# Leaves of six trees instead of four fetched by row, scaled rows of two trees added on VectorE before TensorE turns them, and one TensorE signal for each pair of halves

## The reference

```
h  = patches @ W.T + b                                   # 768 -> 256
x  = layernorm(h);  xn = x / max(rms(x), eps) * g
uv = silu(xn @ uv_w.T)                                   # u 512, v 512, base 128
q, k = rope(base * gamma + beta)
kernel = square(relu((q @ k.T + w_rel[j - i]) / sqrt(128)))
h  = h + x * res_scale + (u * (kernel @ v)) @ o_w.T
y  = layernorm(h)
logits = y @ W_in.T + b_in                               # 8 trees of 255 nodes
current = 0
for d in range(7):                                       # walk down each tree
    current = child of current, right where logits[current] > 0
acts = silu(logits) where the node was visited, else 0
out = h + acts @ W_out.T
```

## Time and profile before

| | us |
|---|---|
| median of 3 runs (least, most) | 2202.95 (2196.44, 2209.55) |
| profiled execution, its own time | 2201.36 |
| its span in the trace | 2199.5 |
| PE busy | 2066.1 (94%) |
| DVE busy | 1621.5 (74%) |
| ACT busy | 1395.2 (63%) |
| POOL busy | 774.1 (35%) |

### The profile page before, as it was taken

How to read it: one execution, slowest core, us unless ns; L and a number is a source line. 1 busy time by engine, 2 the same in 40 slices (tenths; PEclk the granted TensorE clock), 3 DMA queues, 4 the chain that set the end, 5 groups by cost and what they waited for, 6 DMA issues and landing times.

```text
span 2199.5 us, 42461 instructions
## 1 busy us (share of the span) xinstructions
PE 2066.1 (94%) x13256; PEld 1941.8 (88%) x13256; DVE 1621.5 (74%) x4210; ACT 1395.2 (63%) x3085; POOL 774.1 (35%) x905
## 2 busy tenths in 40 slices
PE   6899999999999999999999999999999999999997
PEld 5789889899988898888998898988889988889887
DVE  5678777777777787777777777777777877777775
ACT  5556666666666566566666665666665666656654
POOL 2752333232333333332323333323323233333233
PEclk8999999999999999999999999999999999999999
DMA  5331322222322223222223222222223232222222
GB/s 146 85 94 52 89 73 66 73 76 63 83 71 65 81 55 84 75 64 73 77 62 84 70 73 73 64 75 77 65 70 84 55 85 69 73 73 66 63 67 74
DMA packets 81999, 163.13 MB, mean 74 GB/s; under 512 B 17102, under 2 KB 48048, under 8 KB 81968
## 3 DMA queue, kind: packets, MB, share of 16 engines
q0 software_dynamic: 40960, 103.02, 17.4%
q1 hardware_dynamic: 41008, 59.71, 9.3%
HBM read 148.76 MB, written 13.90 MB: 74 GB/s over the span
## 4 chain that ended last, share of the span: by engine, by line
PE 84%; another core or an unknown queue 5%; ACT 4%; POOL 3%; issue 2%; DVE 1%; DMA 1%; ACTq 0%; POOLq 0%; SPq 0%; DVEq 0%
PE front L1142 10%; PE front L1144 9%; PE front L1143 9%; PE hid_ps L1142 9%; PE hid_ps L1143 9%; PE hid_ps L1144 9%; PE out_acc L1142 6%; PE out_acc L1143 6%; PE out_acc L1144 6%; PE out_acc L1378 4%; PE front L1177 2%; PE front L1184 2%; PE hid_ps L1366 2%; PE hid_ps L1337 2%
## 5 line engine op out<-in xcount | busy, mean ns | idle before, releaser
L474 POOL DMA_INDIRECT leaf_rows<-leaf_table,leaf_at x512 | 532.4, 1040 | 163.9 <-issue 163.4
L453 POOL TENSOR_TENSOR inv_root<-to_root,minus_half 98x8 f32<-98x8 f32 x64 | 111.0, 1734 | 728.3 <-DVE to_root L885 404.6
L528 ACT ACTIVATE hid_hi<-hid 128x392 fp32r<-128x392 f32 (+1 forms) x256 | 177.8, 695 | 237.1 <-PE out_acc L1144 155.4
L1142 PE MATMUL out_acc<-hid_hi,outw_lo 128*128 128x392 f32 x768 | 293.4, 382 | 2.6 <-DVE hid_lo L835 2.3
L1142 PE MATMUL hid_ps<-ffn_x,in_lo 128*128 128x392 f32 x768 | 282.3, 368 | 6.2 <-POOL in_lo L445 5.8
L1143 PE MATMUL hid_ps<-ffn_x,in_hi 128*128 128x392 f32 x768 | 266.3, 347 | 0.0
L1144 PE MATMUL hid_ps<-ffn_x,in_hi 128*128 128x392 f32 x768 | 264.7, 345 | 0.0
L1144 PE MATMUL out_acc<-hid_hi,outw_hi 128*128 128x392 f32 x768 | 264.6, 345 | 0.0
L1143 PE MATMUL out_acc<-hid_lo,outw_hi 128*128 128x392 f32 x768 | 264.4, 344 | 0.0
L473 POOL TENSOR_TENSOR held<-minus_half 98x1 f32<-98x1 f32 x128 | 47.2, 369 | 489.9 <-issue 428.7
L718 ACT ACTIVATE leaf_rows<-leaf_rows,leaf_act 98x256 f32<-98x256 f32 x512 | 218.2, 508 | 0.1
(11 more groups left out here) (140 smaller groups left out, 5808.2 us busy)
## 6 DMA issues: line engine op xcount, KB each, us to landing
x_raw<-x SPq DMA_DIRECT2D x192, 196.0 KB, 2.4
out<-out_stage SPq DMA_DIRECT2D x32, 392.0 KB
leaf_rows<-leaf_table,leaf_at POOLq DMA_INDIRECT x512
leaf_table<-leaf_rows SPq DMA_DIRECT2D x4, 256.5 KB, 4.7
out_stage<-in_w SPq DMA_DIRECT2D x4, 256.0 KB
tok_major<-tok_w SPq DMA_DIRECT2D x3, 256.0 KB, 4.3
late_raw<-out_w SPq DMA_DIRECT2D x6, 128.0 KB
u<-uv_w SPq DMA_DIRECT2D x1, 576.0 KB, 4.2
```

What stands on the lines that cost most here:

```text
L453: pool.tensor_tensor(inv_root[:, 0:size], to_root[:, 0:size], minus_half[:, 0:size], ALU.pow).then_inc(roots_ok, 1)
L474: pool.indirect_dma_start(row_slot(s, g), None, table, bass.IndirectOffsetOnAxis(ap=leaf_at[:, s, g:g + 1], axis=0), element_offset=s * P ...
L528: act.activation(out, src, ACT.Copy).then_inc(done, 1)
L1142: pe.matmul(out, w[1], x_parts[0], start=start, stop=False)
```

## The change

- `GATHERED` is 6 instead of 4, and the rows have 12 slots instead of 8. Two more trees leave out their leaf half in logits and out, and go through `find_leaf`, `leaf_number`, `fetch_rows`, `leaf_dots`, `leaf_silu`.
- Trees of fetched leaves go in couples. ACT scales the rows of the even tree only; DVE's new `merge_rows` (`scalar_tensor_tensor`, 98x256, one for each group) multiplies the odd tree's rows by their activation and adds the even tree's scaled rows; PE's `add_rows` runs once for each couple. A fetch into a slot waits for `rows_merged` where the even tree's rows lay there, for `rows_added` where the odd one's did.
- One signal for a pair of halves: `turn_h`, `turn_back` and `tree_out` raise their semaphore after m = 1 only, `tree_logits` after the last half; `embed` raises `x_used` only after k = 2 and k = 5, so `x_high(3)` waits for `embed(2)` and not for `embed(0)`.
- The lists of all engines are written anew: PE's list starts at another place of the same cycle, and 2 or 3 neighbours are exchanged in many places. POOL's list has `norm_roots` in other places.

```diff
-GATHERED = 4
+GATHERED = 6
-ROW_SLOTS = 8
+COUPLES = GATHERED // 2
+ROW_SLOTS = 12
+X_SIGNALS = (2, 5)
...
                     if GROUPS * (s + 1) > ROW_SLOTS or not first(i):
-                        pool.wait_ge(rows_added, GATHERED * i + s + 1 - ROW_SLOTS // GROUPS)
+                        couple = COUPLES * i + (s - ROW_SLOTS // GROUPS) // 2 + 1
+                        if (s - ROW_SLOTS // GROUPS) % 2 == 0:
+                            pool.wait_ge(rows_merged, GROUPS * couple)
+                        else:
+                            pool.wait_ge(rows_added, couple)
...
                 if k >= XRING or not first(n):
-                    act.wait_ge(x_used, n * XC + k - XRING + 1)
+                    act.wait_ge(x_used, 2 * n + k // XRING)
...
-                dve.wait_ge(h_turned, 2 * (2 * n + which) + m + 1)
+                dve.wait_ge(h_turned, 2 * n + which + 1)
...
+            def merge_rows(i, s):
+
+                if i is None:
+                    return
+                dve.wait_ge(leaf_active, GATHERED * i + s + 1)
+                dve.wait_ge(rows_scaled, GROUPS * (COUPLES * i + s // 2 + 1))
+                for g in range(GROUPS):
+                    one, two = (row_slot(n, g)[:, ROW_IN:ROW] for n in (s - 1, s))
+                    dve.scalar_tensor_tensor(two, two, leaf_act[:, s, g:g + 1], one,
+                                             ALU.mult, ALU.add).then_inc(rows_merged, 1)
...
-                last.then_inc(x_used, 1)
+                if k in X_SIGNALS:
+                    last.then_inc(x_used, 1)
...
-                last.then_inc(done, 1)
+                if m == DC - 1:
+                    last.then_inc(done, 1)
...
-                last.then_inc(logits_ready, 1)
+                if b == halves(t) - 1:
+                    last.then_inc(logits_ready, 1)
...
-                last.then_inc(tree_added, 1)
+                if m == DC - 1:
+                    last.then_inc(tree_added, 1)
...
-                pe.wait_ge(rows_scaled, GROUPS * (GATHERED * i + s + 1))
+                pe.wait_ge(rows_merged, GROUPS * (COUPLES * i + s // 2 + 1))
```

More of the change, by code:

```diff
@@ L1450, in body @@
+                tree_out(i, 0, 0)
+                find_leaf(i, 2)
+                make_base(n)
+                tree_logits(i, 5, 0)
+                tree_out(i, 0, 1)
+                tree_visits(i, 4)
+                make_v(n, 0)
+                make_v(n, 1)
+                make_v(n, 2)
+                tree_out(i, 1, 0)
+                make_v(n, 3)
+                find_leaf(i, 3)
+                tree_out(i, 1, 1)
+                tree_out(i, 2, 0)
+                tree_out(i, 2, 1)
                 if first(n):
@@ new lines, in body @@
+                add_rows(i, 1)
+                tree_logits(i, 6, 1)
+                tree_logits(i, 7, 0)
+                make_u(n, 2)
+                tree_visits(i, 6)
+                find_leaf(i, 5)
+                tree_out(i, 3, 0)
+                make_u(n, 3)
+                mix(n, 0)
+                mix(n, 1)
+                mix(n, 2)
+                tree_out(i, 3, 1)
+                mix(n, 3)
+                tree_logits(i, 7, 1)
+                tree_out(i, 4, 0)
+                tree_out(i, 4, 1)
@@ new lines, in body @@
+                project_o(n, 0, range(0, 3))
+                project_o(n, 0, range(3, EC))
+                project_o(n, 1, range(0, EC))
+                embed(nx, 0)
+                turn_h(n, 1, 0)
+                turn_h(n, 1, 1)
+                embed(nx, 1)
+                embed(nx, 2)
+                tree_visits(i, 7)
+                embed(nx, 3)
+                embed(nx, 4)
+                embed(nx, 5)
+                turn_ffn_x(n, 0)
+                turn_ffn_x(n, 1)
+                tree_out(i, 5, 0)
@@ new lines, in body @@
+                tree_out(i, 5, 1)
+                tree_out(i, 6, 0)
+                turn_h(nx, 0, 0)
+                turn_h(nx, 0, 1)
+                tree_logits(n, 0, 0)
+                tree_logits(n, 1, 0)
+                add_rows(i, 3)
+                tree_visits(n, 0)
+                tree_out(i, 6, 1)
+                tree_visits(n, 1)
+                tree_logits(n, 2, 0)
+                find_leaf(n, 0)
+                tree_logits(n, 3, 0)
+                add_rows(i, 5)
+                tree_out(i, 7, 0)
@@ L1476, in _ @@
+                tree_out(i, 7, 1)
+                turn_xn(nx, 0)
+                turn_xn(nx, 1)
             body(None, None, None, 0)
```

283 lines of the change are left out of this document (117 added, 166 removed).

## The result

The changed kernel takes 2314.76 us, the median of 4 runs (2312.09 to 2317.07), against 2203.7 for the kernel before: a ratio of 1.0505, 95% interval 1.0472 to 1.0539. It is 5% slower where 6% faster was forecast, and 239 us above the predicted 2076.

What follows compares the result with a forecast made beforehand. PE was taken as the bound: 58.8 us of work plus 4.1 of waits make a period of 62.9. 64.8 + 31 x 62.9 + 59.1 + 1.9 = 2075.7, so 2076 us was predicted, range 2020 to 2145.

Steps and rivals of the forecast that it cites:

- PE's work, 58.8: PE's busy time per pair after the change, in us, down from 63.4 with 24 fewer logits and out matmuls.
- turn_xn and make_base: 0.4 each: PE's waits per pair at these two steps, 0.4 us each, bounded by nothing and 1.36.
- How late a signal can be: Lateness of TensorE's signals in the stretch around make_base and make_v, put between 0.04 and 3.07 us.
- The cause of the lateness: TensorE's signals near make_base were said to come 1.8 to 3.1 us late behind the output store.
- Fewer signals: Joined TensorE signals: no gain in ordinary stretches; lateness at make_v taken as 1.0 us, with fewer signals there.
- embed(3) 1.2, embed(5) 0.45, turn_ffn_x 0.3: PE's new waits per pair, in us, at two embed steps and at turn_ffn_x, 1.95 in all.
- make_v 1.3: PE's wait per pair at the matmuls of v, 1.3 us: 0.3 of list plus 1.0 of signal lateness; bounds 0.3 and 3.4.
- Rival B: The clock falls between the embeddings, costing 1.6 us a pair, 2126 us; chance 0.12.
- Rival D: Signals stay 3.07 us late behind the store, make_v waits 2.1 more a pair, 2141 us; chance 0.05.
- Rival C: DVE is the one waited for, with merges at 0.56: 2.5 us more a pair, 2154 us; chance 0.10.
- Rival E: POOL becomes the bound through its 24 fetches; 2358 us at 3.0 us a fetch; chance 0.05.
- The ends: First turning at 64.8 us, 4.9 later because pair 0's roots follow two late splits; 59.1 from the last turning on.

Runs made afterwards that it cites:

- c_before_gate1: The kernel before, with GpSimd fetching tree 1's rows only after make_base of the next pair; 2088.2 us, ratio 0.9446.
- c_gate1_halves: The changed kernel with tree 1's fetch held until make_base, x_used raised after each embed step and a signal after each half; 2114.0 us.
- e_before_sig1: The kernel before with turn_normed's two signals made one, all others as they were; 2283.2 us.
- e_after_half1: The changed kernel with turn_normed's two signals apart again, all others still joined; 2269.0 us.
- a_nostore: The changed kernel with each pair's store cut to one partition of 128; 2311.0 us.
- b_gate1: The changed kernel with GpSimd waiting for make_base before it fetches tree 1's rows; 2167.4 us.
- d_pause: The changed kernel with a GpSimd power of 98x8 ahead of each of the eight fetches of trees 0 and 1; 2564.2 us.
- c_gate1_x: The changed kernel with tree 1's fetch held until make_base and x_used raised after each of the six embed steps; 2116.9 us.

## Why the prediction was wrong

- *PE's work, 58.8*: right in kind, short in size. The 24 matmuls on 392 columns are gone; the windows of c_before_gate1 and c_gate1_halves show 62.8 with 417 and 59.9 with 392 instructions at full clock. Of the 4.6 expected 2.9 show as less busy time; where the rest went is not shown.
- *The step that failed: "turn_xn and make_base: 0.4 each, between nothing and the 43.6 / 32 = 1.36 of make_base now".* make_base's wait measured 159.6 / 31 = 5.1. The upper end was no bound: make_base's wait in the earlier trace rows was made of the same late signals that the prediction let reach 3.07 us at make_v, and it was short because DVE had the first half's signal: without it the kernel before waits 4.97 (e_before_sig1). That is not all. With the two signals apart the changed kernel still waits 4.31 (e_after_half1) where the kernel before waits 1.24, beside a row of eight fetches in both; so 1.4 us of the increase are the joined signal's, and 3.1 came with the rest of the change, in which the first half too gets through only 8.7 us into the row instead of 6.5. Why, no run settles.
- *How late a signal can be, "between 0.04 and 3.07"*: too narrow already for the kernel before. One period behind the earlier trace rows its second half ends at 1097.32 and is heard 4.13 us later:

```profile
1096.76 0.56 PE L1184 MATMUL front<-ident,tok_major 98*128 98x98 f32 x4
...
1101.45 0.62 DVE L899 SCALAR_TENSOR_TENSOR hT<-front,col,hT 128x392 f32<-128x392 f32 x1 [2.95 <-remote]
```

- *The cause of the lateness, "behind a store"*: wrong. The comparison of the earlier trace rows with the earlier trace rows differed in the store and in the fetches, eight in a row against four, and only the store was named. a_nostore, b_gate1 and d_pause show that it is fetches issued back to back; the changed kernel issues eight around turn_normed, as the kernel before did. A row of four made signals late by 1.5 to 1.7 us in the changed kernel (b_gate1, c_gate1_x, c_gate1_halves), but not in that first pair of the kernel before, where a half that ends at 85.05 is heard at 85.09 with an issue under way. What makes the difference is open:

```profile
84.52 0.53 PE L1184 MATMUL front<-ident,tok_major 98*128 98x98 f32 x4
...
85.02 0.97 POOL L474 DMA_INDIRECT leaf_rows<-leaf_table,leaf_at  x1 [0.30 <-issue]
85.09 0.62 DVE L899 SCALAR_TENSOR_TENSOR hT<-front,col,hT 128x392 f32<-128x392 f32 x1 [1.49 <-PE front L1184]
...
86.30 0.97 POOL L474 DMA_INDIRECT leaf_rows<-leaf_table,leaf_at  x1 [0.30 <-issue]
```

- *Fewer signals, "in ordinary stretches I give nothing", and 1.0 instead of 3.07 of lateness at make_v*: the sign was wrong. They cost 44 us in the changed kernel and 251 in the kernel before. By the rule of the Trainium skill ("TensorE: Matmul & The Clock Gate", "The cost: per-tile semaphore tail") they would have saved an estimated 16 us. That rule counts the increments and not how much later a consumer starts, which is what these runs show; the measurement decides.
- *embed(3) 1.2, embed(5) 0.45, turn_ffn_x 0.3*: near in sum. The embed steps measured 41.2 / 31 = 1.3, all but 0.03 of it at embed(3), and turn_ffn_x 0.4 (11.8 / 31). At embed(3) the chain was the one described, but half of the wait has a second cause that the prediction left out: with the signal back, c_gate1_x keeps 0.73, for VectorE's place in its list.
- *make_v 1.3*: 9.9 / 31 = 0.3; the lateness was paid one step earlier.
- *Rival B*: the clock fell, but behind make_base's 5.8 us, not between the embeddings: a clock of 0.93 in the period shown, and 1.00 around embed(3) (1048.5 to 1062.0).
- *Rival D* had the kind right, signals late in spite of the change, and placed it at make_v with 2.1 us. *Rival C* fell: a merge took 160.4 / 384 = 0.42, DVE was busy 56.3 a pair. That this meets the 56.6 worked out is luck: the merges, taken at 0.35, were 0.8 a pair too small, so other terms were as much too large. *Rival E*, GpSimd as the bound, fell as worked out (46% busy, DVE waited 29.9 us for rows), though GpSimd was the cause by another way.
- *The ends*: pair 0's roots came at 28.32, not near 26, because the split ahead of them waited for its weights:

```profile
24.52 0.61 POOL L445 CAST o_hi<-out_stage 128x512 fp32r<-128x512 f32 x1 [23.67 <-DMA out_stage<-o_w]
...
28.32 1.67 POOL L456 TENSOR_TENSOR inv_root<-to_root,minus_half 98x8 f32<-98x8 f32 x1
...
2290.26 0.97 POOL L481 DMA_INDIRECT leaf_rows<-leaf_table,leaf_at  x1 [0.30 <-issue]
2291.02 0.48 PE L1373 MATMUL hid_ps<-decide,toward 128*128 128x392 bf16 x1 [7.25 <-issue]
```

  The roots are 2.3 of the 7.1 us by which the first turning was late. The last two rows are of the tail: PE waits 7.25 and starts as the last pair's last fetch is issued, which looks like the same late signals; no run took them away there. What the rest at both ends is, no run shows.

## What to carry to other kernels

A wait that the trace puts down to "issue" or "remote", with its producer long done, was a late signal here: find what another engine does in that very stretch before calling it small, and look for two causes where two stretches differ in two things. An upper bound read from a row holds only as long as what hides the rest of that wait stays; where a change takes an early signal from beside it, bound the wait by the whole lateness, and read that from many periods. Let the consumer start on the first half, and keep GpSimd's fetches from lying back to back around a step on which TensorE depends: in the kernel before, holding back four of eight fetches gained 5.5%.

## What the runs showed of the hardware

While GpSimd issued eight indirect DMAs one behind the other (one every 1.28 us), other engines heard of TensorE's finished work some 6 us late (find_leaf 6.7, from 1075.64 to 1082.32), in the changed kernel as a rule when the row of issues was over, or up to 1.6 us behind it. The lateness did not depend on the bytes (5.91 us with 2052 and with 256 B a row) nor on the rows (5.82 with 49 instead of 98), was 1.72 with four fetches instead of eight, and 0.25 with 1.7 us of other work ahead of each, which also set them 3.0 us apart. VectorE's own signal was on time in such a stretch: its residual ended at 1030.53 and TensorE started at 1030.59, with an issue under way from 1030.29 to 1031.26. TensorE itself kept starting the matmuls whose inputs were ready. Behind its 5.8 us wait the granted clock was 0.50.
